# Composing the first layer into the weights, four samples at a time, in a chain of four modulated convolutions

## The reference

```
def _layer(x, style, w, b, mw, mb, typ):
    s = style @ mw.T + mb
    weight = SCALE * w * s[:, None, :, None]
    demod = lax.rsqrt(jnp.sum(weight * weight, axis=(2, 3)) + EPS)
    weight = weight * demod[:, :, None, None]
    if typ == 'same':
        out = jax.vmap(_conv_same)(x, weight) + b[None, :, None]
    elif typ == 'upsample':
        out = jax.vmap(_conv_up)(x, weight.transpose(0, 2, 1, 3)) + b[None, :, None]
        out = _blur(out, 2.0 * blur_k, (1, 1))
    elif typ == 'downsample':
        xb = _blur(x, blur_k, (2, 2))
        out = jax.vmap(_conv_down)(xb, weight) + b[None, :, None]
    return out
...
out = x
for i, typ in enumerate(('same', 'upsample', 'same', 'downsample')):
    out = _layer(out, style, weights[i], biases[i], mod_w[i], mod_b[i], typ)
return x + out
```

## Time and profile before

| | |
|---|---|
| median of 3 executions | 167.99 us (167.83 to 169.42) |
| span of the profiled execution | 166.5 us |
| TensorE busy, of the span | 158.8 us, 95% |
| VectorE | 131.8 us, 79% |
| GpSimd | 94.4 us, 57% |
| ScalarE | 56.4 us, 34% |
| mean granted TensorE clock | 0.987 of 2.4 GHz |
| moved by DMA | 17.81 MB, 107 GB/s |

### The profile page before, as it was taken

The page is one execution under the profiler, slowest core; times in us unless marked ns, Lnnn a source line. Parts: engine busy times, 40 slices in busy tenths (PEclk is TensorE's granted clock), DMA queues, the critical chain, the costliest instruction groups (busy, mean ns, idle before and its releaser), DMA issues. The chain is left out here.

```text
span 166.5 us, 8946 instructions
## 1 busy us (share of the span) xinstructions
PE 158.8 (95%) x3975; PEld 146.1 (88%) x3975; DVE 131.8 (79%) x229; ACT 56.4 (34%) x127; POOL 94.4 (57%) x155
## 2 busy tenths in 40 slices
PE   7999999999999999999999999999999999999970
PEld 5687888959789789999899999999999999999960
DVE  7859877788868869778696969696979797969993
ACT  3245561323142332334251514243434334231120
POOL 7209908596493977456373829191919192837530
PEclk9959999999999999999999999999999999999998
DMA  4982000120302204335343445353634242030314
GB/s 119 274 212 14 2 4 4 55 79 4 125 8 65 68 4 126 130 130 190 105 183 118 182 133 186 129 193 111 213 110 145 88 143 101 7 126 4 132 74 180
DMA packets 13990, 17.81 MB, mean 107 GB/s; under 512 B 5216, under 2 KB 5760, under 8 KB 13952
## 3 DMA queue, kind: packets, MB, share of 16 engines
q1 hardware_dynamic: 13888, 17.22, 31.1%
q10 hardware_dynamic: 64, 0.02, 0.1%
HBM read 8.85 MB, written 8.39 MB: 104 GB/s over the span
## 5 line engine op out<-in xcount | busy, mean ns | idle before, releaser
L190 POOL TENSOR_TENSOR Hw<-Hw 128x192 f32<-128x192 f32 x15 | 9.0, 598 | 50.8 <-DVE Hw L885 50.8
L546 PE MATMUL p_m<-uu,Hw 64*64 64x128 f32 x992 | 31.6, 269 | 0.0
L546 PEld LDWEIGHTS p_m<-uu,Hw 64*64 64x64 f32 x992 | 29.4, 132 | 0.1
L466 PE MATMUL p_lo<-xin,w0s 64*64 64x259 f32 x384 | 27.7, 406 | 0.1
L309 POOL COPY Hw<-Hw 64x896 f32<-64x896 f32 x15 | 25.8, 1722 | 1.0
L466 PE MATMUL p_le<-xin,w0s 64*64 64x260 f32 x384 | 26.3, 389 | 0.0
L511 PE MATMUL p_le<-R_sb,F_st 64*64 64x128 f32 (+2 forms) x768 | 25.8, 266 | 0.3 <-issue 0.3
L536 PE MATMUL p_m<-u,Hw 64*64 64x256 f32 x384 | 25.4, 375 | 0.0
L896 DVE TENSOR_TENSOR uu<-u 128x516 f32<-128x516 f32 x32 | 24.3, 796 | 1.4
L911 DVE TENSOR_TENSOR e_sb<-p_lo,s_sb 128x512 f32<-128x512 f32 x16 | 11.1, 696 | 16.8 <-PE p_lo L546 16.6
L511 PEld LDWEIGHTS p_le<-R_sb,F_st 64*64 64x64 f32 x768 | 23.3, 133 | 1.1 <-issue 0.9
(11 more groups left out here) (140 smaller groups left out, 217.8 us busy)
## 6 DMA issues: line engine op xcount, KB each, us to landing
xin<-in_x_dram SPq DMA_DIRECT2D x32, 256.0 KB, 3.3
out_dram<-ot SPq DMA_DIRECT2D x32, 256.0 KB, 2.4
wn<-in_L_cond_weights_dram SPq DMA_DIRECT2D x1, 192.0 KB, 3.5
mwn<-in_L_cond_mod_w_dram SPq DMA_DIRECT2D x1, 128.0 KB, 2.2
xe<-in_x_dram SPq DMA_DIRECT2D x2, 56.0 KB, 7.7
cn<-in_cond_dram ACTq DMA_DIRECT2D x1, 16.0 KB, 2.0
bn<-in_L_cond_mod_b_dram ACTq DMA_DIRECT2D x1, 1.0 KB
bn<-in_L_cond_biases_dram ACTq DMA_DIRECT2D x1, 1.0 KB
```

Source lines behind the costliest of these rows:

```text
L466: ins = pe.matmul(bank[h * C:(h + 1) * C, s, 0:n], w0s[p % 2][rows, k, :], xin[p % NX][rows, i0:i0 + 2 * n - 1:2], start=(k == 0), stop=(k ...
L546: ins = pe.matmul(bank(h)[s * C:(s + 1) * C], tap(p, h, s, blk), moving(slice(h * C, (h + 1) * C), s, k), start=(k == 0), stop=(k == len(b ...
```

## The change

Layer 0 is multiplied into the taps as well. The 32 samples go in eight quads of four; a sample has an index i (row half in one step, column half in the next) and j, so that each of the four tiles carries its own sample and each tap has one place. `place_H`, `sum_taps`, `make_diffs`, `make_uu`, `layer0_odd` and `layer0_even` are gone.

`compose_R` now makes five blocks, `compose_H` seven, and the new `compose_T` the nine taps (eight in one bank, the ninth in another). `evac_T` copies them out with layer 0's style as scale, `add_ident` adds a multiple of the identity to the centre tap (the input's own path, which `add_x` did), and `sum_blocks` makes ten sums of taps. The samples are applied straight to the input in SBUF: `make_d` and `make_dd` (VectorE) and `make_dx` (GpSimd) make its differences at both levels of the splitting, and all products have 256 columns: `product_a2` three blocks of four matmuls, `product_bc2`, `product_a13` and `product_bc1` five each, `product_bc3` four. `product_a2` reads the input at a step of four elements. `make_s`, `make_e` and `finish` scale by the demodulation while they add, and `finish` writes the output at a step of four.

The demodulation of layers 2 and 3 is split from that of layers 0 and 1. GpSimd no longer waits for `wsum` and `e2`: after the weights have landed it makes four copies, then `make_dx(0)`, then the blurred weights. Loads and stores have 512 KB; the first three quads are stored during the third. The edge is one position wider. Of the diff the new lines that matter here stand below; the functions that it removes are printed above.

```diff
+        def add_ident(eng, q):
+            wait(eng, T_ident, q)
+            eng.tensor_tensor(di_sb[:], ident2[:].unsqueeze(1).to_broadcast([P, 2, C]),
+                              pvec[:, W_ID, 2 * q:2 * q + 2].unsqueeze(2).to_broadcast([P, 2, C]), ALU.mult)\
+                .then_inc(di_made, 1)
+            eng.wait_ge(T_evac, 4 * (q + 1))
+            eng.wait_ge(di_made, q + 1)
+            w = Tw[q % NW][:, 4]
+            eng.tensor_tensor(w, w, di_sb[:], ALU.add).then_inc(T_ident, 1)
+        def sum_blocks(eng, q):
+            w = Tw[q % NW]
+            eng.wait_ge(T_ident, q + 1)
+            eng.tensor_tensor(w[:, B_S:B_S + 4], w[:, 8:0:-2], w[:, 7:0:-2], ALU.add).then_inc(T_sums, 1)
+            blk = 2 * C
+            a = w[:]
+            eng.tensor_tensor(w[:, B_U:B_U + 4].rearrange("p (a b) j c -> p a b (j c)", b=2),
+                              view(a, 8 * blk, ((-4 * blk, 2), (-blk, 2), (1, blk))),
+                              view(a, 6 * blk, ((-4 * blk, 2), (-blk, 2), (1, blk))), ALU.add).then_inc(T_sums, 1)
+            eng.wait_ge(T_sums, 3 * q + 1)
+            eng.tensor_tensor(w[:, B_SS:B_SS + 2], w[:, B_S:B_S + 4:2], w[:, B_S + 1:B_S + 4:2], ALU.add).then_inc(T_sums, 1)
+        def make_dx(eng, q):
+            eng.wait_ge(padded, NX)
+            eng.wait_ge(x_loaded[q % NX], 32 * (q // NX + 1))
+            wait(eng, bc2_done, q - 1)
+            a = xin[q % NX][:]
+            eng.tensor_tensor(dx_sb[q % 2][:], view(a, 1, ((XW, 2), (4, 2), (4, NI))),
+                              view(a, 3, ((XW, 2), (0, 2), (4, NI))), ALU.subtract).then_inc(dx_made, 1)
         block = ctx.enter_context(nc.Block())
...
+            for l, to, name in ((2, V_st, "V_st"), (0, W0_st, "W0_st")):
+                of = wn[:, l].rearrange("o i k -> o k i")
+                for h in range(2):
+                    pool.tensor_copy(to[h * C:(h + 1) * C], of).then_inc(copied[name], 1)
+                    pool.wait_ge(copied[name], h + 1)
+            make_dx(pool, 0)
...
+            for q in range(QUADS):
+                if q + 1 < QUADS:
+                    make_dx(pool, q + 1)
+                if q == 1:
+                    finish_z()
+                if q + 1 < QUADS:
+                    add_ident(pool, q + 1)
+                    sum_blocks(pool, q + 1)
+                if q == 0:
                     finish_y()
...
+            for q in range(QUADS):
+                if q + 3 < QUADS:
+                    sp.wait_ge(a2_done, q + 1)
+                    for j in range(2):
+                        load(q + 3, j)
+                for r in (range(LATE + 1) if q == LATE else range(q, q + 1) if q > LATE else ()):
+                    for i in range(2):
+                        store(r, i)
             for s in range(NO_T):
...
+            def compose_R(q, bank):
+                pe.wait_ge(A_made, 2 * (q + 1))
+                if q > 1:
+                    pe.wait_ge(T_evac, 4 * q)
+                for b in range(K):
+                    for i in range(2):
+                        for j in range(2):
+                            rows = slice(j * C, (j + 1) * C)
+                            ins = pe.matmul(bank[i * C:(i + 1) * C, j, b * C:(b + K) * C], V_st[rows, K - 1 - b, :],
+                                            A_sb[q % 2][rows, i], start=(b == 0), stop=(b == K - 1),
+                                            skip_group_check=True)
                 ins.then_inc(R_done, 1)
...
+            def compose_H(q):
+                pe.wait_ge(R_evac, 2 * (q + 1))
+                if q > 0:
+                    pe.wait_ge(T_evac, 4 * q - 2)
+                for f in range(NF):
+                    par = f % 2
+                    n = 3 - par
+                    to = (f + par) // 2
+                    for i in range(2):
+                        rows = slice(i * C, (i + 1) * C)
+                        for j in range(2):
+                            ins = pe.matmul(p_k[j * C:(j + 1) * C, i, to * C:(to + n) * C], F_st[rows, f, :],
+                                            R_sb[q % 2][rows, j, par::2], start=(f == 0), stop=(f == NF - 1),
+                                            skip_group_check=True)
                 ins.then_inc(H_done, 1)
...
+            def compose_T(q):
+                pe.wait_ge(H_evac, 2 * (q + 1))
+                wait(pe, T_evac, 4 * q)
+                if q == 0:
+                    pe.wait_ge(copied["W0_st"], 2)
+                    pe.wait_ge(R_evac, 4)
+                if 2 <= q <= 3:
+                    pe.wait_ge(made["e_read"], 2 * (q + 1))
+                for k, first, n in ((2, 0, NH), (1, 1, NH), (0, 2, NH - 1)):
+                    for i in range(2):
+                        for j in range(2):
+                            rows = slice(j * C, (j + 1) * C)
+                            pe.matmul(p_h[i * C:(i + 1) * C, j, first * C:(first + n) * C], W0_st[rows, k, :],
+                                      H_sb[rows, i, 0:n], start=(k == 2), stop=(k == 0), skip_group_check=True)
+                for i in range(2):
+                    for j in range(2):
+                        rows = slice(j * C, (j + 1) * C)
+                        ins = pe.matmul(p_k[i * C:(i + 1) * C, j, NH * C:(NH + 1) * C], W0_st[rows, 0, :],
+                                        H_sb[rows, i, NH - 1], start=True, stop=True, skip_group_check=True)
...
+            def part(q, bank, c0, blocks, moving):
+                for n, blk in enumerate(blocks):
+                    for i in range(2):
+                        rows = slice(i * C, (i + 1) * C)
+                        for j in range(2):
+                            ins = pe.matmul(bank[j * C:(j + 1) * C, i, c0:c0 + NQ], Tw[q % NW][rows, blk, j, :],
+                                            moving(rows, j, n), start=(n == 0), stop=(n == len(blocks) - 1),
+                                            skip_group_check=True)
                 return ins
...
+            def product_a2(q):
+                bank = p_c[q % 2]
+                pe.wait_ge(T_sums, 3 * (q + 1))
+                pe.wait_ge(x_loaded[q % NX], 32 * (q // NX + 1))
+                wait(pe, y02_made, 2 * q)
+                a = xin[q % NX]
+                part(q, bank, 0, (B_SS, B_SS + 1, 0),
+                     lambda rows, j, n: a[rows, j, 3 + 4 * n:3 + 4 * n + 4 * NQ - 3:4]).then_inc(a2_done, 1)
+            def product_bc2(q):
+                bank = p_c[(q + 1) % 2]
+                pe.wait_ge(dx_made, q + 1)
+                wait(pe, y13_made, 2 * q)
+                a = dx_sb[q % 2]
+                part(q, bank, 0, (B_S, B_S + 2, 0), lambda rows, j, n: a[rows, j, 0, n:n + NQ])
+                part(q, bank, NQ, (B_S + 1, B_S + 3), lambda rows, j, n: a[rows, j, 1, n:n + NQ]).then_inc(bc2_done, 1)
+            def product_a13(q):
+                bank = p_c[q % 2]
+                pe.wait_ge(d_made, q + 1)
+                pe.wait_ge(t_made, 2 * (q + 1))
+                def odd(of):
+                    return lambda rows, j, n: d_sb[rows, j, of, 1 + 2 * n:1 + 2 * n + 2 * NQ - 1:2]
+                part(q, bank, 0, (B_U, B_U + 2, 0), odd(0))
+                part(q, bank, NQ, (B_U + 1, B_U + 3), odd(1)).then_inc(a13_done, 1)
+            def product_bc1(q):
+                bank = p_c[(q + 1) % 2]
+                pe.wait_ge(dd_made, q + 1)
+                pe.wait_ge(s_made, 2 * (q + 1))
+                part(q, bank, 0, (8, 4, 0), lambda rows, j, n: dd_sb[rows, j, 0, 0, n:n + NQ])
+                part(q, bank, NQ, (6, 2), lambda rows, j, n: dd_sb[rows, j, 0, 1, n:n + NQ]).then_inc(bc1_done, 1)
+            def product_bc3(q):
+                bank = p_c[q % 2]
+                pe.wait_ge(e_made, 4 * (q + 1))
+                part(q, bank, 0, (7, 3), lambda rows, j, n: dd_sb[rows, j, 1, 0, n:n + NQ])
+                part(q, bank, NQ, (5, 1), lambda rows, j, n: dd_sb[rows, j, 1, 1, n:n + NQ]).then_inc(bc3_done, 1)
...
+            for q in range(QUADS):
+                product_a2(q)
+                if 0 < q < QUADS - 1:
+                    compose_H(q + 1)
+                if q == 0:
+                    pe.wait_ge(made["e_read"], 2)
                     pe.wait_ge(made["c"], 2)
...
+            def evac_T(q):
+                act.wait_ge(T_done, q + 1)
+                wait(act, bc3_done, q - NW + 1)
+                for j in range(2):
+                    act.activation(Tw[q % NW][:, 8, j], p_k[:, j, NH * C:(NH + 1) * C], ACT.Copy,
+                                   scale=pcol(W_S0, 2 * q + j)).then_inc(T_evac, 1)
+                for j in range(2):
+                    act.activation(Tw[q % NW][:, 0:8, j], p_h[:, j, 0:8 * C].rearrange("p (a c) -> p a c", c=C), ACT.Copy,
+                                   scale=pcol(W_S0, 2 * q + j)).then_inc(T_evac, 1)
...
+            def make_d(q):
+                dve.wait_ge(padded, NX)
+                dve.wait_ge(x_loaded[q % NX], 32 * (q // NX + 1))
+                wait(dve, a13_done, q)
```

(101 more changed lines are left out.)

845 lines of the change are left out of this document (294 added, 551 removed).

## The result

The changed kernel takes 244.22 us (median of 4, 244.05 to 245.24) where the kernel before takes 168.56 in the same series (4 runs, 167.83 to 169.42): 1.446 times as long (95% interval 1.436 to 1.456), where 164.0 was forecast. Its profiled execution has a span of 242.4 us.

A forecast was written before the change was run, and what follows sets the result against it. TensorE's columns were taken to bound the kernel. First product at 34.0, plus 124.1 to VectorE's end, plus 4.4 of end: 162.5 us of span; the median lies 1.5 above, 164.0 us against 167.99, range 159 to 171.

The forecast's parts named there:

- the stores: Loop: three quads of stores in the third quad, 3 MB at 277 GB/s, 11 us, fit a quad and cost nothing.
- The read at a step of four: `product_a2` in the loop: 0.07 us added a quad, bounds 0 and 0.2; 1 us went to the range.
- The write at a step of four: `finish` in the loop: taken as free; at double price mostly hidden by VectorE's slack, 5 us for the range.
- The loop's columns: TensorE per quad: 36,096 columns against 39,360 for two pairs, 8% fewer; a full quad 15.45 us against 17.1.
- First product to VectorE's end: Loop, all eight quads: 124.1 us, 12.3 less than before.
- `make_A(0)`: Start: VectorE's step comes between 11.2 and 16.4 us, taken as 15.5 beside GpSimd's work; 12.17 before.
- the rivals of the chain: Loop: chain after `product_a13` has no slack; four `make_e` taking 3.7 instead of 2.75 us give 170.5; chance 0.14.
- the lock in the loop: Rival: VectorE's pointer-scalar instructions wait for GpSimd's sums, some 3.7 us lost a quad, 186 us; chance 0.04.
- three signs of being wrong: Quads over 16 us apart; granted clock low after 16 us; first product before 31 or after 37.
- paragraph on the lock: Start: VectorE and GpSimd share SBUF ports under an exclusive lock; L309 and L311 agree, 0.93 us longer beside L948.
- The clock's rival: Start: clock stays at 1.2 GHz until the first product, larger groups take 8 us more, 172 us; chance 0.10.
- The tail: End: last two 512 KB stores, 1 MB at 277 GB/s, finish 4.4 us after VectorE, where it was 2.4.

The follow-up runs named there:

- e5: Changed kernel with the loads of the fourth and later quads issued from ScalarE's queue, stores as they are: 244.88 us.
- e1: Changed kernel with each store cut in two, one sample each: 178.51 us, ratio to before 1.058; profiled execution 177.19 us, span 175.4.
- e3: Split-store changed kernel with `product_a2` reading at a step of one instead of four (wrong values): 169.1 us against 177.19.
- f2: Split-store changed kernel with ScalarE copying `product_a2`'s columns together one quad ahead, output right: 168.08 us.
- f3: Split-store changed kernel with both repairs, columns copied together for `product_a2` and `finish` writing at a step of two: 165.6 us, ratio to before 0.984.
- f1: Split-store changed kernel with `product_bc1`, `product_bc3` and `make_e` writing interleaved, so `finish` writes at a step of two: 175.61 us.
- g1: Split-store kernel with both step repairs, plus GpSimd held back until `e2` is made: 163.98 us, ratio to before 0.976.

## Why the prediction was wrong

**The step that failed is the stores.** The prediction's "the three quads of stores in the third quad (3 MB at 277 GB/s, 11 us) fit a quad" and "They cost nothing here" took a rate from the earlier trace rows, where the 128 rows of each store belong to two neighbouring samples and are addressed as one list of rows, for stores whose destination is two separate samples. Measured: 53 GB/s. 8.39 MB at that rate are 158 us, and from the first store (73.67) to the end it was 168.7. Nor did the loads go "past the stores on SyncE's queue": those of the seventh and eighth quad stand behind them. That mattered to the loop (12 us, e5), but not to the time. Of the 79.9 us between the forecast span (162.5) and the measured one (242.4), this step is 67.0 (after to e1). No rival named it: the new form of address is part of the change, and it was not priced from both sides though no row of the trace has it.

**The read at a step of four** was taken at 0.07 us a quad, the near row's excess, with three times that, 0.2, as the upper bound. Measured: 1.40 a quad (e1 to e3), twenty times the value taken and seven times the bound. Step two and step four are not on one line: `product_a13` at step two costs 386 ns a record against 377, `product_a2` at step four 632. **The write at a step of four** was taken as free, with double price as the bound. Measured: 1168 ns against 740, some 0.6 times dearer, inside the bound; once the read is repaired it costs 0.37 us a quad (15.74 to 15.37) and 3.4 us of span in all (f2 to f3), where the bound had 5. Together the two are 12.5 us (175.4 to 162.9).

The Trainium skill, page "SBUF — State Buffer", section "Specifications (TRN2)", states lines of 16 bytes and at least two accesses on each for the full rate. Four fp32 fill a line, so a step of two still has two accesses on it and a step of four has one. By that rule step four leaves the full rate where step two does not; TensorE's 632 against 386 ns agree, and VectorE's and ScalarE's figures do, while GpSimd's `make_dx`, at 2.4 us for 1,032 elements, runs at the pace that the earlier trace rows gave for it.

**What held.** The loop's columns at 0.42 ns: 15.45 forecast for a full quad, 15.37 in f3. First product to VectorE's end: 124.1 forecast, 123.7 in f3 (33.36 to 157.06). `make_A(0)` 15.5, measured 15.12; first product 34.0, measured 33.85. Neither chain set the loop: `make_e` took 0.74 to 0.77 each, also beside GpSimd's sums, so the rivals of the chain and of the lock in the loop fell. The start's result is partly made of two errors that cancel: `style2` did not wait for `make_dx(0)`, whose load landed later than reckoned (two operations for `e1` did, for 1.6 us), and the clock was low longer, to nearly 20 us, so that R(0) took 1.9 where 0.97 was reckoned. With the quads 17.2 us apart, two of the prediction's three signs of being wrong are there. In its paragraph on the lock, L309 is 0.89 us longer than L311 (1.82 against 0.93), not 0.93. The clock's rival was right as a mechanism, not as a case: in the changed kernel it is back at the upper level by 20 us, long before the first product. The tail was forecast at 4.4 us and is 5.8 in f3: its last 1 MB moves at 111 to 311 GB/s over some 5 us where 277 was taken; why is open. With the stores and both steps mended the sum, 162.5 us of span, comes near f3's 162.9. That is in part luck: the start is 0.6 us shorter than forecast, the loop 0.4 shorter and the tail 1.4 longer, and f3's profiled execution is its shortest; its median of 165.6 lies 1.6 above the forecast of 164.0. What was forecast is the repaired kernel, not this one.

## What to carry to other kernels

Price a DMA by its address pattern as well as its bytes: when an edit changes which rows a store or load covers, no row of the old form bounds its rate, and the first thing to read in the profile is GB/s beside the share of engines busy. Ask of each new step through memory whether the trace has that very step; a cheap step of two says nothing of a step of four. An end that is set by a queue stays hidden while the engines look busy, so compare the last instruction of the last engine with the end of the span.

## What the runs showed of the hardware

A store of 512 KB to two separate samples runs at 53 GB/s, with 0.13 of 16 engines busy; stores of one sample each, two in its place, run at 295 GB/s alone (end of e1), with 0.93 busy. An fp32 matmul of 64x256 read at a step of four takes 630 ns a record with four tiles at work, 386 at a step of two, 377 at one; writing PSUM at a step of two it takes 378 (f1). VectorE's fp32 write at a step of four takes 1.17 us for 508, at a step of two 0.77, in a row 0.74; ScalarE's read at a step of four takes 1.2 us for 516. In g1 the granted clock was 0.50 to 0.55 (1.2 GHz) in every window from 8 to 22 us; before it fell TensorE had the small groups of the preparation, while it was low the blurred taps on two tiles, R, transposes and the beginning of H(0), and it was 1.00 again from 22 us on.
